# Scaling the rows of a feed-forward output by 1/rms: from one fused VectorE operation to a ScalarE scaling and a GpSimd product

## The reference

```python
logits = x @ router_w + router_b
full_w = softmax of the two largest logits, zero elsewhere
expert_out = silu(x @ expert_w[e] + expert_b[e])        # e = 0..7
combined = sum over e of full_w[e] * expert_out[e]
y = x + combined @ proj_w + proj_b                      # x: the layer-normed rows
rms = sqrt(mean(y * y) + 1e-6)
return norm_w * (y / rms)                               # 0.5 of it is added to the stream
```

## Time and profile before

| | us |
|---|---|
| median of 3 runs (897.51 to 898.15) | 897.56 |
| span of the profiled execution | 895.1 |
| f1, from the first instruction | 0 to about 170 |
| attention | about 170 to 742 |
| f2 | about 742 to 895.1 |

### The profile page before, as it was taken

The page is one execution under the profiler, slowest core; times in us unless marked ns, Lnnn a source line. Parts: engine busy times, 40 slices in busy tenths (PEclk is TensorE's granted clock), DMA queues, the critical chain, the costliest instruction groups (busy, mean ns, idle before and its releaser), DMA issues. The chain is left out here.

```text
span 895.1 us, 17013 instructions
## 1 busy us (share of the span) xinstructions
PE 835.9 (93%) x4848; PEld 716.8 (80%) x4848; DVE 699.7 (78%) x1824; ACT 520.8 (58%) x1252; POOL 582.9 (65%) x442
## 2 busy tenths in 40 slices
PE   5998988677999999999999999999999997999995
PEld 4676766566989999999899999999999886777774
DVE  6789989899776776776866866867777797688976
ACT  3654544445675765755765865765756754444452
POOL 3657756377587787687777777787787702545743
PEclk9999999978999999999999999999999999999998
DMA  9053253410212311312311312312312100000001
GB/s 301 1 177 90 86 200 153 130 36 12 49 24 59 105 23 35 102 27 59 94 33 37 94 23 70 94 23 47 89 28 48 25 1 29 1 1 24 24 1 47
DMA packets 26673, 55.98 MB, mean 63 GB/s; under 512 B 3568, under 2 KB 9840, under 8 KB 25104
## 3 DMA queue, kind: packets, MB, share of 16 engines
q1 hardware_dynamic: 26640, 55.59, 21.4%
HBM read 22.02 MB, written 12.58 MB: 39 GB/s over the span
## 5 line engine op out<-in xcount | busy, mean ns | idle before, releaser
L1048 POOL TENSOR_TENSOR at_ql<-at_rot,at_qh 128x512 fp32r<-128x512 f32 x62 | 79.8, 1288 | 99.7 <-ACT at_qh L1270 99.7
L1287 ACT ACTIVATE at_pr<-at_sm,at_low 128x512 f32<-128x512 f32 (+3 forms) x256 | 140.5, 555 | 1.3 <-DVE at_low L1135 1.3
L1293 ACT ACTIVATE at_pth<-at_pt 128x512 fp32r<-128x512 f32 (+1 forms) x192 | 95.8, 525 | 76.0 <-PE at_pt L1447 75.0
L601 ACT ACTIVATE f_s<-f_ex,f_cols 128x512 f32<-128x512 f32 x128 | 84.5, 686 | 91.6 <-PE f_ex L749 53.6
L292 POOL TENSOR_TENSOR f_acc<-f_acc,f_u 128x512 f32<-128x512 f32 x68 | 100.5, 1503 | 44.5 <-DVE f_u L481 27.8
L1145 DVE TENSOR_SCALAR at_pr<-at_pr,at_inv 128x128 f32<-128x128 f32 (+3 forms) x256 | 113.3, 504 | 2.3
L1135 DVE CUSTOM_DVE_ANT_0 at_sm<-at_sc,at_mask 128x512 f32<-128x512 f32 (+3 forms) x256 | 109.8, 484 | 2.5 <-issue 2.4
L1150 DVE TENSOR_TENSOR at_ptl<-at_pt,at_pth 128x512 fp32r<-128x512 f32 (+1 forms) x192 | 108.6, 592 | 1.7 <-ACT at_pth L1293 1.7
L1057 POOL TENSOR_TENSOR at_rot<-ga,cos 128x512 f32<-128x512 f32 x78 | 104.2, 1336 | 4.1 <-POOL at_ql L1048 2.4
L1063 POOL TENSOR_TENSOR at_rot<-at_rot,gc 128x512 f32<-128x512 f32 x78 | 101.4, 1300 | 8.1 <-POOLq L1080 2.1
L1447 PE MATMUL at_pt<-ident,at_pr 128*128 128x128 f32 x640 | 96.0, 278 | 7.9 <-DVE at_pr L1145 6.0
(11 more groups left out here) (211 smaller groups left out, 2248.9 us busy)
## 6 DMA issues: line engine op xcount, KB each, us to landing
gc<-ga SPq DMA_DIRECT2D x160, 128.0 KB, 2.3
ga<-in_attn_w SPq DMA_DIRECT2D x4, 1280.0 KB, 8.1
attn_split<-gb SPq DMA_DIRECT2D x4, 1280.0 KB, 9.8
attn_split<-gc SPq DMA_DIRECT2D x4, 1280.0 KB, 12.2
gb<-attn_split SPq DMA_DIRECT2D x8, 512.0 KB, 4.1
at_wo<-attn_split SPq DMA_DIRECT2D x8, 512.0 KB, 3.9
x<-in_x SPq DMA_DIRECT2D x4, 512.0 KB, 9.2
e_raw<-in_expert_w SPq DMA_DIRECT2D x8, 256.0 KB, 6.9
```

Source lines behind the costliest of these rows:

```text
L1287: act.activation(pr[h % 2][:, cols], sm[h % 2][:, cols], ACT.Exp, bias=low[h % 2][:, i:i + 1], scale=-1.0, accum_out=tot[h % 2][:, i:i + 1 ...
L1293: act.activation(pth[h % 2][:, cols], pt[(NF * h + k) % 2][:, 0:FLEN[k]], ACT.Copy).then_inc(hi_done, 1)
```

## The change

`scale_rows` leaves VectorE. ScalarE now multiplies each tile of y by its 1/rms in place, behind the silu of expert 2, and GpSimd multiplies all of y by n_w in one operation of 128x1024 before it adds y to x, with a new semaphore `yn_done` between its two operations. GpSimd also waits once, at the start, for `consts`, the semaphore that says that n_w was halved.

```diff
@@ gpsimd
             def add_rows(i):
                 pool.wait_ge(xn_done, BT * i + BT)
+                pool.tensor_tensor(y[:], y[:], n_w.unsqueeze(1).to_broadcast([P, BT, D]), ALU.mult).then_inc(yn_done, 1)
+                pool.wait_ge(yn_done, i + 1)
                 xb = x[:, bass.ds(i * BT, BT), :]
                 pool.tensor_tensor(xb, xb, y[:], ALU.add).then_inc(x_done, 1)
...
             residual(0)
+            pool.wait_ge(consts, 1)
             body(0, False, True)
@@ vector
-            def scale_rows(i):
-                dve.wait_ge(rr_done, i + 1)
-                for t in range(BT):
-                    dve.scalar_tensor_tensor(out=y[:, t, :], in0=y[:, t, :], scalar=rr[:, t:t + 1], in1=n_w,
-                                             op0=ALU.mult, op1=ALU.mult).then_inc(xn_done, 1)
...
-                    if e == 2 and prev:
-                        scale_rows(i - 1)
@@ scalar
+            def scale_rows(i):
+                act.wait_ge(rr_done, i + 1)
+                for t in range(BT):
+                    act.activation(y[:, t, :], y[:, t, :], ACT.Copy, scale=rr[:, t:t + 1]).then_inc(xn_done, 1)
...
                 for e in range(2, E):
                     silu(i, e)
+                    if e == 2 and prev:
+                        scale_rows(i - 1)
```

More of the change, by code:

```diff
@@ L147, in ffn_phase @@
         chi_done, clo_done, y_done, yadd_done, sq_done = (sem(n) for n in ("chi_done", "clo_done", "y_done", "yadd_done", "sq_done"))
-        rms, rr_done, xn_done, x_done = (sem(n) for n in ("rms", "rr_done", "xn_done", "x_done"))
+        rms, rr_done, xn_done, yn_done, x_done = (sem(n) for n in ("rms", "rr_done", "xn_done", "yn_done", "x_done"))
         if out is not None:
```

## The result

The changed kernel takes **902.14 us** in the median of 4 runs (901.14 to 903.38); the kernel before, on the same chip in the same minutes, 897.53 (896.48 to 898.15, 4 runs). The ratio is 1.0054 with a 95% interval of 1.0040 to 1.0068: slower by 4.6 us. The profiled execution has a span of 900.7 us where that of before had 895.1. The prediction was 902.7 (898.8 to 906.1), slower with a chance of 0.80.

A forecast was written before the change was run, and what follows sets the result against it. GpSimd's queue with VectorE's two-SBUF-input operations, then the gating, was taken to bound TensorE. Terms 1.4 + 1.0 - 0.3 + 1.0 + 1.6 + 0.5 = +5.2 us gave 902.7 us, range 898.8 to 906.1.

The forecast's parts named there:

- Removed from VectorE: First feed-forward: four operations, 4.9 us per block, go; VectorE gains 2.7 us at expert 3, TensorE's vanished wait returns at the gating.
- VectorE's is the cover: Both feed-forwards: GpSimd's queue, which the change lengthens, is what counts; VectorE's queue only covers it.
- Rule against row: Skill's rule to leave elementwise work to VectorE, against measured row: slower by 0.5 us per block, 3 in all.
- The queue of GpSimd in f1: First feed-forward, blocks 1 and 2: GpSimd's longer queue ends later, delaying the gating +0.7 us per block (0.4 to 1.2).
- Blocks 1 and 2 of f2: Second feed-forward, middle blocks: same queue reckoning without L451, +0.5 us each (0.3 to 0.7), passed on to TensorE at L769.
- Last block of f1: First feed-forward's end: expert 5's product comes 2.3 us earlier, but holds give most back: -0.3 us (-2.3 to +0.7).
- Last block of f2: Second feed-forward's end: a TensorE wait shrinks 1.1 us, then sums held by GpSimd's product and addition: +1.0 us (0 to 1.6).
- The clock: TensorE: one more low-clock stretch behind the first feed-forward's gating stall at 88.8, grown to 3.7 us: +1.6 us (0 to 1.7).
- The clock does not fall once more: No added low-clock stretch, as stalls of 1.8 to 2.3 us went both ways: 899.2 to 900.7 us; chance 0.20.
- Gains and losses cancel: GpSimd's idle time and holds nearly absorb the product, last blocks keep part of their gains: 896.5 to 899 us; chance 0.09.
- VectorE decides: faster: Product falls into time when GpSimd would wait anyway, so VectorE's relief counts: about 8 us faster, 889.5 us; chance 0.06.
- ScalarE blocks: ScalarE waits longer for `rr`, expert 3's silu comes late and TensorE stalls at expert 5: 908 us; chance 0.07.

The follow-up runs named there:

- square of four: Four kernels compared: before 897.5 us, only VectorE relieved (no GpSimd product) 887.2, only the product added 911.1, both 902.1.
- three reorderings: Changed kernel, GpSimd's product and addition behind the sum of 4 and 5: 902.37 us; residual before all sums: kernel before 893.58, changed kernel 901.37.
- the fastest kernel: Kernel before with unscaled y in PSUM, the fused operation one expert earlier, and GpSimd's residual in front of the sums in middle blocks: 887.65 us.

## Why the prediction was right, point by point

**The sum** came out within 0.6 us of the median, and its parts add up to 5.2 against 5.4 in the table of places. The forecast's case is the one that happened.

**The range** was not added up as it says. All high ends together give +8.7, not +8.5. The low ends without the clock give -0.9 with the last block of f1 at its -2.3, and +1.1 with it at -0.3; neither the +1.2 of the range nor the +1.6 of the first rival comes out of the parts. The measured 902.14 lies well inside either way.

**Removed from VectorE** ("it is worth nothing" for the stall at 73.22; gain 2.7 us at the product of expert 3): right for the changed kernel, where VectorE waits 2.14 us at once for `select`. But the kernel without its product shows that this relief is worth 10.3 us once nothing takes it away. "VectorE's is the cover" was too strong: in the kernel before VectorE and GpSimd bound the block together. (Under *Rule against row* the prediction also has 4 x 0.43 us for VectorE's four unheld operations and, two sentences on, 1.9 us; the row says 4 x 0.479 = 1.9.)

**Added to ScalarE**: four activations take 1.71 us in block 1 of f1 (reckoned 1.3 to 2.0), 498 ns in the mean, and no cost shows in the run that adds them alone (ratio 1.0002, 0.9985 to 1.0019).

**Added to GpSimd**: 2.38 us unheld, as taken from the earlier trace rows. The semaphore behind it, put at under 0.1 us, shows 0.19 us of idle time in the middle blocks and 0.07 in the last block of f1.

**The queue of GpSimd in f1**: +0.7 per block was forecast and +1.0 came, inside its bounds, but *by the other engine*. The step that failed is the sentence "which leaves VectorE no later than that". I reckoned GpSimd held for 3.2 to 4.0 us and its sum of 4 and 5 later by 0.4 to 1.2; it was held for some 2.0 and came 0.8 earlier. It was VectorE that stood in the turns: 5.56 us for the two sums and 2.62 for the subtraction, against 3.37 and 1.48, together 3.3 us more, of which 1.0 is left at the gating. I had named the turns and had not followed VectorE's side of them to the end. The right size here was in part luck.

**Blocks 1 and 2 of f2**: +0.5 was forecast each, +0.35 and +0.32 came, and by the forecast way: GpSimd's sum of 4 and 5 ends 0.33 later, and VectorE waits for it.

**Last block of f1**: the term of -0.3 was mis-sized, it measured -0.94 from the block's experts and -1.07 from its first projection matmul (31.65 and 32.72 us; -0.92 where the change is made in that body alone). L418 and L411 are held as reckoned, 1.87 and 2.88 us.

**Last block of f2**: +1.0 forecast, +1.19 measured (+1.22 alone). The chain written out in the prediction puts TensorE's start at 884.3 (883.26 + 1.0); counted in the old time it came at 884.5 (888.12, less the 3.67 us by which the block's first projection matmul was late).

**The clock**: +1.6 was forecast for one more low stretch behind the first gating stall, and 1.64 was measured between that stall and the next experts. The size is right. The reason given, the stall's new length of 3.7 us, is not shown, and one run speaks against its being needed: with the change in the last bodies alone block 1 of f1 is as before and so is its stall (1.8 us), yet the profile has

```profile
88.00:92.00 4.00, 3.13 (x18) 0.78 1.00 425
92.00:96.00 4.00, 4.00 (x20) 0.80 0.44 184
```

and from block 2's first projection to its gating takes 36.0 us where before it took 34.4. So such a stretch costs 1.6, but whether one comes there differs between executions of the same instructions. Yet more time at the lower clock does come with the change, and not in one execution only: the mean granted clock was 0.971 to 0.973 in all four runs of the changed kernel and 0.975 to 0.979 in 23 of the 26 runs of the kernel before beside the last experiments. Which stall brings it is not shown. Of the 4.6 us I can therefore hold only some 3 to the holds by themselves; the rest is low clock whose cause stays open, and that it came to the 1.6 that were forecast is in part luck.

**The signs** named in the prediction came, with two exceptions. The sum of 4 and 5 did not end later in f1, as said above. And one sign of being wrong did appear: the attention's length changed by over 0.5 us (586.1 for 587.1). It tells nothing here, since that length runs from 582.0 to 587.6 us over the profiles of all kernels with nothing edited in it.

**The rivals.** "The clock does not fall once more" did not happen in the profiled execution. "Gains and losses cancel" and "VectorE decides: faster" did not happen; the latter's condition, the product falling into time that GpSimd has to spare, comes nearest in the kernel with the product taken out, at 887.2 (889.5 was its price). "ScalarE blocks", priced at 908, is excluded by its own run. The rule weighed there, the Trainium skill's GPSIMD Engine Reference, section 4.1, gave the sign and 3 us in all; the runs give 4.6, and by another way: the square of four shows 13.5 to 14.9 us for the product and 8.9 to 10.3 for the relief, two large effects of opposite sign of which the difference is left.

## What to carry to other kernels

Before work is moved between VectorE and GpSimd, count for each GpSimd instruction which VectorE operations with two SBUF inputs are issued beside it: a short one behind a long one costs up to the long one's length, and where a second long one is queued, two short ones in a row can cost both. What that is worth depends on the place: here the product cost 15 us in all for 15.2 us of its own busy time, but 2.6 us in a middle block of f1 and 0.5 in one of f2. Putting one input of the fused operation into PSUM, and issuing it one expert earlier, gave 8.3 us with no work moved to another engine. And a move of such a collision is worth nothing unless there is idle time where it goes: two of three reorderings gave nothing clear of noise.

## What the runs showed that was not expected

**Low clock without a longer stall.** The number of stretches at half clock within f1, each about 3.4 us and worth 1.6 to 1.7, was one in the profile of before, two in that of the change, one without the product, three with the product added, and two in the fastest kernel (887.65 us), whose gating stalls are only 1.1. Counted in single profiles it does not order the kernels. The mean granted clock over all runs does in part: 0.979 to 0.981 without the product, 0.971 to 0.973 with the change, 0.964 to 0.975 with the product added; but it is 0.976 to 0.978 in the fastest kernel. The Trainium skill (TensorE: Matmul & The Clock Gate, Part 1) says that what the gate looks at is not aligned to the kernel's start. The two profiles with the same code in block 1 of f1 and unlike clocks behind it fit that, and no run here tests it.

**The attention phase varies by itself.** From its first matmul to the second gating transposes of f2 (at 789.57 in the profile of before), so with f2's block 0, it took 618.6 us in the profile of before and 618.8 in that of the change, but 613.7 with the product moved late, 614.5 with half of it and 616.2 with the change in the last bodies alone, although nothing in it was edited. Single executions of one kernel spread accordingly (895.14 is the median of twelve between 890.59 and 896.93). A profile's span is therefore compared here place by place, and times by medians; the cause of the spread stays open. The clock alone is not it: from 170 to 225 us the profile of before and that with the product moved late both have some 20 us at half clock.
